# Recommendation tower with three cross layers: the sum that ends a tile of layer 1 made in two halves, the second behind the next tile's first group

## What is computed

```
for W in filters:                       # f0, f1, f2: (39*39,128), (128*39,128), (128*39,128)
    z   = einsum('bfd,bgd->bfgd', x0, xk).reshape(b, f*g, d)
    cur = einsum('bpd,pm->bmd', z, W)
    outs.append(cur); xk = cur
z = sum(concatenate(outs, axis=1), axis=-1)
h = relu(concat(z, dense_ctx) @ W_top1 + b1); h = relu(h @ W_top2 + b2); y = h @ W_top3
```

## Time and profile before

| | us |
|---|---|
| median of 3 runs | 726.49 |
| the three runs | 724.42, 726.49, 2229.46 |
| the profiled execution | 722.3 |
| its span, first to last instruction | 720.5 |
| mean granted TensorE clock | 0.991 |

### The profile page before, as it was taken

How to read it: one execution, slowest core, us unless ns; L and a number is a source line. 1 busy time by engine, 2 the same in 40 slices (tenths; PEclk the granted TensorE clock), 3 DMA queues, 4 the chain that set the end, 5 groups by cost and what they waited for, 6 DMA issues and landing times. The chain is left out here.

```text
span 720.5 us, 11962 instructions
## 1 busy us (share of the span) xinstructions
PE 647.5 (90%) x2571; PEld 473.9 (66%) x2571; DVE 537.1 (75%) x1152; ACT 524.1 (73%) x1846; POOL 451.6 (63%) x537
## 2 busy tenths in 40 slices
PE   0789899999999898989899999979898999989988
PEld 0257677676767676767677676757676777765663
DVE  1556769697878787887969697867879696988880
ACT  2157678787888787777788787857777787887762
POOL 6857976868595868686776859485867635101330
PEclk9989999999999999999999999999999999999999
DMA  7551321222222130413022222203130230301000
GB/s 200 119 115 55 60 64 44 61 52 61 52 40 74 36 78 10 97 15 88 18 63 49 60 52 60 53 10 101 11 89 18 64 91 0 106 1 40 30 1 0
DMA packets 58221, 40.29 MB, mean 56 GB/s; under 512 B 36625, under 2 KB 41055, under 8 KB 58202
## 3 DMA queue, kind: packets, MB, share of 16 engines
q1 hardware_dynamic: 52376, 38.73, 21.7%
q0 software_dynamic: 5120, 1.29, 2.1%
q10 hardware_dynamic: 706, 0.06, 0.1%
HBM read 38.13 MB, written 1.94 MB: 56 GB/s over the span
## 5 line engine op out<-in xcount | busy, mean ns | idle before, releaser
L607 ACT ACTIVATE parts<-psa,x0c 128x128 f32<-128x128 f32 x1536 | 440.6, 409 | 101.4 <-PE psa L756 101.1
L503 DVE SCALAR_TENSOR_TENSOR parts<-psd,x0c,parts 128x128 f32<-128x128 f32 x960 | 266.6, 343 | 107.7 <-PE psd L756 65.2
L485 DVE TENSOR_REDUCE cur<-parts 128x128 f32<-128x3072 f32 x64 | 214.6, 3353 | 25.1 <-ACT parts L607 16.7
L752 PE MATMUL psa<-w1h,x1h 128*128 128x512 f32 x384 | 177.4, 462 | 11.8 <-ACT parts L607 9.6
L333 POOL DMA_INDIRECT emb<-tables,idx x140 | 135.5, 968 | 45.3 <-POOL idx L329 25.0
L756 PE MATMUL psa<-w1h,x1l 128*128 128x512 f32 x384 | 152.8, 398 | 0.0
L753 PE MATMUL psa<-w1l,x1h 128*128 128x512 f32 x384 | 152.8, 398 | 0.0
L341 POOL TENSOR_TENSOR pairs<-x0t,pairs 117x512 f32<-117x512 f32 (+1 forms) x105 | 133.8, 1292 | 7.8 <-DMA pairs<-x_rows 7.0
L752 PE MATMUL psd<-w1h,x1h 128*128 128x512 f32 (+1 forms) x256 | 104.9, 410 | 32.7 <-DVE parts L503 32.5
L752 PEld LDWEIGHTS psa<-w1h,x1h 128*128 128x128 f32 x384 | 72.8, 190 | 46.7 <-ACT parts L607 20.8
L756 PE MATMUL psd<-w1h,x1l 128*128 128x512 f32 (+1 forms) x256 | 98.0, 383 | 0.0
(11 more groups left out here) (82 smaller groups left out, 537.6 us busy)
## 6 DMA issues: line engine op xcount, KB each, us to landing
pairs<-x_rows SPq DMA_DIRECT2D x113, 156.0 KB
pairs<-x_rows SPq DMA_DIRECT2D x30, 234.0 KB
x0t<-x_rows SPq DMA_DIRECT2D x16, 234.0 KB
emb<-tables,idx POOLq DMA_INDIRECT x140
x_rows<-emb SPq DMA_DIRECT2D x14, 72.0 KB
wt_sb<-w_top SPq DMA_DIRECT2D x1, 768.0 KB, 7.3
parts<-w SPq DMA_DIRECT2D x1, 704.0 KB, 4.7
x_rows<-emb SPq DMA_DIRECT2D x14, 40.0 KB
```

Source lines behind the costliest of these rows:

```text
L485: dve.tensor_reduce(cur1[:, t % 2, :], parts[:, t % 2, :, :].rearrange("p k (j m i) -> p m (k j) i", m=M, i=2), AX.XY, ALU.add).then_inc(c ...
L503: op = dve.scalar_tensor_tensor(acc, y[:, M * j:M * j + M], x0c[:, t, GF * g + j:GF * g + j + 1], acc, ALU.mult, ALU.add)
L607: op = act.activation(lanes(dst, j), y[:, M * j:M * j + M], ACT.Copy, scale=x0c[:, t, GF * g + j:GF * g + j + 1])
L752: pe.matmul(y[:, 0:n], hi, w1h[:, c], start=True, stop=False)
```

## The change

`finish_tile` becomes two halves of 64 output columns each. The first is where the whole sum was, with the same three waits. The second stands behind the accumulations of the next tile's first d group, ahead of `low_part(b, 3)` in tile 0 and of `sum_cur0` in tile 2. It has no wait of its own and raises `c1_ready`. The last tile's second half stands behind all blocks.

```diff
-            def finish_tile(b, t):
+            def sum_half(t, first, end):
+
+                terms = parts[:, t % 2, :, :].rearrange("p k (j m i) -> p m (k j) i", m=M, i=2)
+                return dve.tensor_reduce(cur1[:, t % 2, first:end], terms[:, first:end, :, :], AX.XY, ALU.add)
+
+            def finish_first_half(b, t):
 
                 T = b * TILES + t
                 dve.wait_ge(act_prods, b * NA + A_OFF[t + 1])
                 dve.wait_ge(acc_steps, b * ND + D_OFF[t + 1])
                 if t >= 2 or not starts(b):
                     dve.wait_ge(g2_done, T - 1)
-                dve.tensor_reduce(cur1[:, t % 2, :],
-                                  parts[:, t % 2, :, :].rearrange("p k (j m i) -> p m (k j) i", m=M, i=2),
-                                  AX.XY, ALU.add).then_inc(c1_ready, 1)
+                sum_half(t, 0, M // 2)
+
+            def finish_second_half(t):
+
+                sum_half(t, M // 2, M).then_inc(c1_ready, 1)
...
                         op.then_inc(acc_steps, 1)
+                        if n == 0 and (t or not starts(b)):
+                            finish_second_half((t - 1) % TILES)
                         if (t, n) == (0, 0):
                             low_part(b, TILES - 1)
...
-                    finish_tile(b, t)
+                    finish_first_half(b, t)
...
             block_of(NBLK - 1, False)
+            finish_second_half(TILES - 1)
```

## The result

The changed kernel is **slower: 738.9 us median (734.4 to 742.7) against 726.1**, a ratio of 1.018 with a 95% interval of 1.012 to 1.024. The profiled execution took 734.43 us, 732.6 in the span, 12.1 more than before. 727.8 was predicted, in a range of 716 to 742. So the sign and the range hold, and the size doesn't: 12.8 us against 2.3. One of the four runs of the kernel before (2229.46 us) and one of the four of the changed kernel run again in experiment 2 (1065.41) were far slower than the others and stand outside the ratios.

What follows compares the result with a forecast made beforehand. TensorE, 90% busy, loses time in waits, while the chain through GpSimd's gather sets the block. Turns +7.0, block 14 -1.2, last block -3.6, last sum +0.1 make +2.3 us: 727.8 us, range 716 to 742.

Steps and rivals of the forecast that it cites:

- The cost of a half: VectorE's sum of 64 outputs takes 1.75 us, a slot of 1.67; two take 0.07 more than the whole.
- Steps 1, 3 and 4: VectorE's tiles 1 to 3 and GpSimd's gather held by group 4: the gather starts 0.58 us later each turn.
- Step 2: ScalarE's `high_part` follows `sum_cur0`, so all its work up to group 8 moves 0.63 us later.
- Step 5: TensorE's waits on VectorE shrink; it reaches group 8 of tile 0 1.18 us earlier, then stands about 2.3 us.
- the falling clock: Rival: TensorE's clock falls in the new gap at group 8, 1.43 us a turn, +17.2 in all 12; chance 0.17.
- The same: Outcome within some 2% (14.5 us) of no change; chance 0.80, against faster 0.07 and slower 0.13.
- The ends: Where GpSimd sets nothing: block 14's tile 0 gains 1.2 us, the last block's four tiles 3.6.
- Start: Block 0's gathers find their counts passed, so block 1 stays: 0, with 1 us to either side.
- The Trainium skill's two rules: VectorE waiting for an empty pipe would add 0.24 us a turn, 2.9 in all; idle time halves TensorE's clock.

Runs made afterwards that it cites:

- experiment 2: Changed kernel with two extra layer 0 matmuls ahead of group 8: 0.9984, 722.7 us; with one: 0.9995, 717.8 us; unaltered, run again: 1.0182.
- experiment 3: GATHERS_FROM (the gate: which VectorE group a row number waits for) 5, not 6: changed kernel 0.9522, 690.6 us; kernel before 0.9823, 711.6 us.
- experiment 5: Changed kernel cut into 96 and 32 outputs, not 64 and 64: with two extra layer 0 matmuls 0.9920; with GATHERS_FROM at 5 0.9454.

## Why the prediction was right in part and wrong in part

- **The cost of a half** (1.75) and the 0.07 us of halving: right, 1.748 and 0.06.
- **Steps 1, 3 and 4, a turn 0.58 us longer:** right. Each start fell within 0.02 us, a turn with the clock up took 39.18 us where 39.2 was given, and experiment 3 shows the gate to be the link.
- **Step 2:** the delay is right, the cause is only half of it. `low_part(0)` behind group 6 binds ScalarE as much as `sum_cur0` does; moving the sum alone gained 0.13 us, moving both 0.73.
- **Step 5, TensorE stands for 2.3 us:** the gap is right (2.09 by the row, 3.11 - 0.86 = 2.25 from start to start). What it costs is where the prediction failed. The sum took it at nothing, and the falling clock was kept as a rival with 0.17, with the argument that "here TensorE is full on both sides". That didn't protect it: it fell in 10 of 12 turns. The missing term is 9 x 1.66 + 2.86 = 17.8 us, which is more than the 12.8 us of the result. The rival's size was nearly right, 1.43 us a turn. The rival was also said to decide "once a gap is long enough, in whichever turns that is"; gaps of 2.09 us did and didn't.
- **The range holds by luck.** With that term added the forecast would have been about 745 us, outside the range. Between the two profiled executions it was offset by what nobody forecast: a start 3.0 us shorter, a gather that came late in the kernel before and cost 4.2 us there, and ends that gained 0.8 more than the sum gave them. "The same", within 2%, was given 0.80; the interval of 1.012 to 1.024 lies on both sides of that line.
- **Why 1.66 and not 1.43:** in the late gather's turn the clock had fallen 0.2 us ahead of the restart and was back 3.1 us behind it, so a part of the low stretch passed in idle. In the changed kernel's turns nearly all of it falls on work: 1.59 us at 371.28, where it began with the restart, 1.65 at 291.24, where it began 1.5 us behind it.
- **The ends:** -5.6 us where -1.2 - 3.6 was given; a tile of the last block takes 7.40 and not 7.5, which is 0.4 of the 0.8.
- **Start:** taken as 0 with 1 us to either side; it moved by 3.0, and by as much between other kernels.
- **The Trainium skill's two rules.** By the sentence of the Trainium skill, "VectorE: DVE Perf Modes", section "The DRAIN you can't avoid", that the prediction took up, the turn would have been 0.24 us longer still. The same section goes on that a next instruction which isn't held starts earlier, and the prediction left that out. The rows agree with this second part: a half of 1.75 us at 316.44 and the next instruction at 318.11, 1.67 later, and a turn of 39.18. The rule on the clock in the Trainium skill, "TensorE: Matmul & The Clock Gate", Part 1, by which idle time halves it at moments that don't start with the kernel, agrees with equal gaps of 2.09 us after which it fell in one turn and not in the next. The rival deserved more than 0.17.

## What to carry to other kernels

A stall that is removed ahead of a second, later gate isn't won: it gathers into one longer gap at that gate, and on TensorE a gap may cost clock on top. Before a change, look for the wait that ends last in a turn, across all engines (here GpSimd's, through a pacing constant of one group), and price the gap it leaves by what the trace shows after its longest waits. The same change can be a loss of 1.8% or a gain of 3.1% by that one constant.

## What the runs showed that was not expected

- The clock can fall after the engine is back at work: at 291.24 TensorE restarts at full clock, and from 292.58 its matmuls take nearly twice as long. In other turns it falls at the restart (371.28) or ahead of it.
- In the changed kernel idle of 2.09 to 3.40 us ahead of group 8 brought it down in 22 of 24 turns; 2.21 did in one turn of experiment 5. Idle of 1.24 to 1.26 us did in none of 11, but neither did 2.52 and 3.11 us in two single turns; 0.86 us of needless matmul in the gap, 14 times or 12 us of work, was worth some 1.9%.
- A GpSimd gather behind a held row number starts 0.83 to 0.84 us after VectorE's last product (321.01 + 1.12 to 322.96 in the changed kernel, 312.05 to 312.89 before); where nothing held the row number the gather has 0.15 us of idle ahead of it and not 0.48. So a second hold costs twice: for what it waits, and 0.33 us for coming out of it.
